# Retention of a two-layer decoder: rotated keys, state and queries in 16-bit parts, with the split and the state's spreading moved between engines

## The chip, the cores and the metric

The kernel runs on one core of one Trainium2 chip. The metric is the device time of one execution in microseconds. Of the kernel before there are three runs, and a profiled execution with its trace.

## The reference

A decoder of two layers on x of 2 x 1024 x 256 with a context of 2 x 154 x 192: a table-based attention, a cross attention and a mixture of experts; then a retention, a headed cross attention and a feed-forward part with sign weights. The change is in the retention alone. With 16 heads, key dimension 16 and head dimension 32 it computes, for tokens m and n of one sequence (positions m, n; `decay` per head):

```python
q = x @ q_w + q_b;  k = (x @ k_w + k_b) * SCALING;  v = x @ v_w + v_b;  g = x @ g_w + g_b
qr = q * cos + rotate_every_two(q) * sin            # the same for kr
qk = einsum('bhmd,bhnd->bhmn', qr, kr) * mask       # mask: tril(exp((m - n) * decay)) / sqrt(its row sum)
qk = qk / clip(abs(qk.sum(-1)), 1)
out = einsum('bhmn,bhnd->bhmd', qk, vr)
out = (out - mean) / sqrt(var + 1e-5)
out = (silu(g) * out) @ o_w + o_b
```

## The kernel before

`retention` runs 16 tiles of 128 tokens (`NT = 16`), 8 to a sequence (`TB = 8`). Within a tile the scores are formed and masked; what earlier tiles of the sequence give comes through a state `us` (per head 16 x 33: 32 values and a column of ones), decayed by `keep` and spread by head into `u`. Each engine has its own queue, written out by hand: a loop over steps s = -2 to 18 in which every function works on the tile that its argument names. Semaphores named after what is done (`rot_done`, `v_done`, ...) tie the engines together. Precise 32-bit work is done either with fp32 operands or with two fp16 parts, high and low, and three products.

What the queues hold per step, in order:

- TensorE: `score(s, 0)` (half of the heads, into `pss`), `weigh(s - 1)` (state product with `u`, attention by values, into `pso`), `qk(s + 2)` (projection into `psq`), `score(s, 1)`, `turn_qk(s + 1, 0)` (queries transposed into `ptr`), `output(s - 3)`, `turn_qk(s + 1, 1)` (keys), `values(s + 1)` (projection into `psv`), `delta(s)` (the tile's part of the state, into `psd`), `turn_z(s - 2)`, `turn_x(s + 4)`, `gates(s - 1)` (projection into the same `psv`). `pss` has one buffer, so `score(s, 1)` waits for `low(s, 0)`, and `score(s + 1, 0)` for `low(s, 1)`.
- VectorE: `low(s, 0)`, `x_center(s + 5)`, `gate(s - 2)`, `rotate(s + 2)`, `low(s, 1)`, `centre(s - 1)`, `state(s)`, `add(s - 3)`, `z_low(s - 2)`, `values_low(s + 1)`, `x_low(s + 4)`, and statistics for the next stage in some steps.
- ScalarE: `high(s, 0)`, `squares(s - 1)`, `high(s, 1)`, the copies of the turned queries and keys (L2859), `values(s + 1)` (a fp16 and a fp32 copy of the values, L2867 and L2868), `z_high(s - 2)`, `x_high(s + 4)`, `silu(s - 1)` (in place in `psv`, L2879).
- GpSimd: two selects for each half of the scores (`mask`, L2686), `power(s - 1)` (L2705), `expand(s)` (L2695: the state into `u`, four copies of it with all heads but one set to zero).

The rotation (L2779 to L2785) turns 256 queries and 256 keys per token with `cos` and `sin` and writes fp32 into `rot`, with 16 zeros behind each 16 values. Before, the scores (L2922) and the state's products (L2937, L3022) have fp32 operands. `values` runs on ScalarE; `values_low` subtracts the fp16 copy from the fp32 copy `v32`, both in SBUF, and `gates` waits for `v_done`, that is for ScalarE's second copy.

## Time and profile before

| | |
|---|---|
| median of three runs | 1028.42 us (1023.22 to 1030.12) |
| the profiled execution | 1025.94 us, of it 1024.1 us span |
| TensorE busy | 874.4 us, 85% of the span |
| VectorE busy | 784.2 us, 77% |
| ScalarE busy | 615.7 us, 60% |
| GpSimd busy | 372.5 us, 36% |
| mean granted TensorE clock | 0.949 |
| the retention | from about 506 to 720 us of the span |

Busy time is the time in which an engine's instructions ran; TensorE's are pipelined, so its rows overlap their successors and the distance between two starts is what a row costs. In a row of the timeline the first number is the start, the second how long the row lasted; "[1.29 <-ACT r_att L2852]" is idle time of the engine ahead of the row and what ended it. The names are `r_` with the tile's name of the code, `ra_` for tiles prepared ahead of the stage. On VectorE and ScalarE too neighbours overlap by about 0.1 us.

### The profile page before, as it was taken

Reading aid. Unit: us, or ns where it says so; the run is one execution under the profiler, and the core shown is the slowest. Engines: PE = TensorE matmul, PEld = TensorE weight load, DVE = VectorE, ACT = ScalarE, POOL = GpSimd, SP = SyncE. Lnnn points to the kernel's source line nnn. Section 1 sums busy time; section 2 is a strip of 40 time slices with the busy share of each in tenths; the row PEclk is TensorE's granted clock in tenths of the full one; section 3 lists DMA queues with packets and bytes.
Section 4 is the critical chain, followed back from the end, with each engine's and each line's share of the span. In section 5 each row is a group of like instructions: output and inputs, shape, how many; then the busy total and the mean of one; then the engine's idle time right before and its main releaser. Section 6 shows DMA issues by size and latency. Waiting matters only on the chain. (4 is left out here: it accounts for less than half of the span.)

```text
span 1024.1 us, 22180 instructions
## 1 busy us (share of the span) xinstructions
PE 874.4 (85%) x8762; PEld 579.5 (57%) x8762; DVE 784.2 (77%) x1460; ACT 615.7 (60%) x1108; POOL 372.5 (36%) x326
## 2 busy tenths in 40 slices
PE   1386878788488899999689999998799998999997
PEld 0122323232246555565356777776689975778786
DVE  8899989833788899887678899887577886667443
ACT  5578789887476554452155555554578865656431
POOL 1043435321247140000246667666144641224220
PEclk9998889898679899999899999999799999999999
DMA  5403232320420030000120000000200000000000
GB/s 148 83 1 48 36 54 32 48 37 1 135 72 1 2 135 1 1 2 1 58 111 1 3 2 2 2 3 2 73 2 2 2 1 1 2 12 11 12 22 31
DMA packets 21670, 30.47 MB, mean 30 GB/s; under 512 B 6000, under 2 KB 17982, under 8 KB 20416
## 3 DMA queue, kind: packets, MB, share of 16 engines
q1 hardware_dynamic: 18816, 26.44, 11.2%
q10 hardware_dynamic: 2752, 2.62, 0.9%
q8 instruction: 70, 1.15, 0.5%
q14 instruction: 32, 0.26, 0.1%
HBM read 18.56 MB, written 2.10 MB: 20 GB/s over the span
## 5 line engine op out<-in xcount | busy, mean ns | idle before, releaser
L589 ACT ACTIVATE t_pT<-t_sc 128x1536 f32<-128x1536 f32 x96 | 136.7, 1454 | 28.8 <-PE t_sc L696 28.5
L269 POOL TENSOR_SCALAR_AFFINE_SELECT t_pT<-t_pT 128x512 f32<-128x512 f32 x64 | 75.9, 1206 | 167.4 <-ACT t_pT L589 167.3
L696 PE MATMUL t_sc<-t_qk 32*128 32x512 f16 (+3 forms) x1152 | 89.1, 365 | 47.4 <-DMA t_qk<-t_sin_parts 26.6
L696 PEld LDWEIGHTS t_sc<-t_qk 32*128 32x128 f16 x1152 | 37.1, 99 | 107.0 <-issue 50.4
L2686 POOL TENSOR_SCALAR_AFFINE_SELECT r_att<-r_att 128x1024 f16<-128x1024 f16 x64 | 69.5, 1108 | 66.2 <-DVE r_att L2726 66.2
L717 PE MATMUL t_ot<-t_pT,t_v 128*17 128x512 f32 (+3 forms) x768 | 81.3, 535 | 11.3 <-DVE t_ou L433 5.1
L1983 PE MATMUL c_pso<-ck_VO,c_pT 128*128 128x256 f16 x480 | 55.0, 273 | 1.4 <-DVE c_pT L1824 1.4
L2726 DVE TENSOR_TENSOR r_att<-r_pss,r_att 128x1024 f16<-128x1024 f32 x32 | 39.1, 1221 | 20.2 <-ACT r_att L2852 20.2
L1983 PEld LDWEIGHTS c_pso<-ck_VO,c_pT 128*128 128x128 f16 x480 | 46.3, 98 | 6.7 <-DVE c_pT L1824 1.6
L2268 ACT ACTIVATE m_sg<-m_psg 128x512 f32<-128x512 f32 x32 | 19.1, 596 | 51.6 <-PE m_psg L2311 51.5
L2852 ACT CAST r_att<-r_pss 128x1024 f16<-128x1024 f32 x32 | 32.4, 1012 | 28.0 <-PE r_pss L2922 28.0
L1894 ACT ACTIVATE c_pt<-c_pss,c_mx 128x154 f32<-128x154 f32 x128 | 48.4, 415 | 1.1 <-DVE c_mx L1807 1.1
L2332 PE MATMUL m_acc<-gw_down,m_hp 128*128 128x256 f16 x384 | 47.2, 273 | 1.9 <-DVE m_hp L2224 1.4
L2948 PE MATMUL r_psv<-ra_w,ra_xT 128*128 128x512 f16 x192 | 46.8, 380 | 1.0 <-ACT r_v L2868 1.0
L2705 POOL TENSOR_TENSOR r_sm<-r_sm,ra_sm 128x16 f32<-128x16 f32 x16 | 46.3, 2895 | 3.6 <-DVE r_sm L2767 2.0
L717 PEld LDWEIGHTS t_ot<-t_pT,t_v 128*17 128x17 f32 x768 | 17.5, 102 | 51.8 <-issue 37.6
L1774 POOL TENSOR_TENSOR c_pn<-c_pt,c_tot 128x208 f32<-128x208 f32 x16 | 24.1, 1507 | 58.3 <-DVE c_tot L1814 58.3
L2332 PEld LDWEIGHTS m_acc<-gw_down,m_hp 128*128 128x128 f16 x384 | 36.9, 98 | 12.4 <-DVE m_hp L2224 2.0
L2922 PEld LDWEIGHTS r_pss<-r_qkT 32*128 32x128 f32 x512 | 31.0, 186 | 13.6 <-issue 11.2
L2922 PE MATMUL r_pss<-r_qkT 32*128 32x128 f32 x512 | 37.1, 283 | 1.0 <-DVE r_att L2726 1.0
L2859 ACT COPY r_qkT<-r_ptr 128x512 f32<-128x512 f32 x32 | 18.8, 588 | 29.7 <-PE r_ptr L2996 29.7
L1824 DVE TENSOR_TENSOR c_pT<-c_pst,c_pT 128x512 f16<-128x512 f32 (+1 forms) x48 | 28.7, 598 | 10.3 <-ACT c_pT L1905 9.4
(593 smaller groups left out, 2408.7 us busy)
## 6 DMA issues: line engine op xcount, KB each, us to landing
t_qk<-t_cos_parts SPq DMA_DIRECT2D x24, 128.0 KB, 5.4
t_qk<-t_sin_parts SPq DMA_DIRECT2D x24, 128.0 KB, 7.0
x<-in_x ACTq DMA_DIRECT2D x4, 512.0 KB, 7.3
out_x<-x SPq DMA_DIRECT2D x8, 256.0 KB, 2.1
r_rcos<-in_ret_cos SPq DMA_DIRECT2D x1, 1280.0 KB, 9.1
r_rsin<-in_ret_sin SPq DMA_DIRECT2D x1, 1280.0 KB, 10.6
t_qk<-t_cos_parts SPq DMA_DIRECT2D x16, 64.0 KB, 2.7
gw_raw<-in_gateT SPq DMA_DIRECT2D x1, 1024.0 KB, 7.6
```

What stands on the lines that cost most here:

```text
L269: last = g.affine_select(out=blk, in_=blk, compare_op=ALU.is_ge, fill=0.0, base=0, pattern=[[0, 4], [1, P]], channel_multiplier=-1)
L589: a.activation(pT[:, at:at + 3, :].rearrange("p a s -> p (a s)"), sc[s % 2][:], ACT.Exp, scale=CURVE * CURVE / math.sqrt(2 * DH)).then_inc ...
L696: last = t.matmul(sc[s % 2][:, 512 * k + at:512 * k + at + w], qk[r, g % 3, 1, of_k, P * i:P * i + P], qk[r, g % 3, 0, of_q, q0:q0 + w], s ...
L717: last = t.matmul(ot[j][32 * h:32 * h + DH + 1, 512 - w:512], v1[:, b, 4 * c + h, i, :], pT[:, (4 * slot + h) % RING, at:at + w], start=be ...
L1894: last = a.activation(pt[:, q, h, :], pss[:, k, n * CTX:n * CTX + CTX], ACT.Exp, bias=mx[:, q, 3 * k + n:3 * k + n + 1], scale=1.0, accum_ ...
L1983: last = mm(pso[:, 0:D], l, r, start=(n == 0), stop=(n == len(todo) - 1))
L2332: last = mm(acc[:, j, :], hp[:, k, ph_, P * j:P * j + P], dw[:, pw, D * e:D * e + D], start=(e == 0 and j % 2 == 0 and ph_ + pw == 0), sto ...
L2686: last = g.affine_select(out=blk, in_=blk, compare_op=ALU.is_ge, fill=0.0, base=0, pattern=[[0, 8], [1, P]], channel_multiplier=-1)
L2705: g.tensor_tensor(sm[:, q, 2, :], sm[:, q, 1, :], ahead.sm[:, 4, 0:1].broadcast_to((P, HR)), ALU.pow).then_inc(pow_done, 1)
L2726: v.tensor_tensor(att[:, t % 2, 1, 2 * j:2 * j + 2].rearrange("p h g m -> p (h g m)"), pss[:].rearrange("p j m -> p (j m)"), att[:, t % 2, ...
L2922: last = mm(pss[:, j, P * g:P * g + P], qkT[r, q, 1, g, :], qkT[r, q, 0, g, :], start=(g == 0), stop=True, skip_group_check=True)
L2948: last = mm(d, l, r, start=(i == 0), stop=(i == len(todo) - 1))
```

## The change

- The rotation's sum stays in `psq` in fp32. ScalarE copies it as fp16 into `rot` (`rotated_high`), VectorE subtracts that and writes the rest, fp16, beside it (`rotated_low`): 16 high values and 16 low ones stand where 16 values and 16 zeros stood. GpSimd writes a third plane of `rot` with the keys' two parts exchanged (`swap`).
- Scores are two fp16 products per head in place of one in fp32: keys (high, low) and keys (low, high), each with queries (high, low). Twelve fp16 transposes replace eight in fp32, and the keys' copy from `ptr` is 1024 wide.
- The state is split by GpSimd into fp16 parts `us16` (`split_state`), and `expand` moves from GpSimd to ScalarE: four operations with a scale per partition. The state product in `weigh` is two fp16 products for one in fp32; `delta` has four fp16 products for one in fp32.
- `v32` is gone. `values_low` reads `psv` itself, stands ahead of `state` and not behind `z_low`, and `gates` and the next `values` wait for `vlo_done`, where they waited for `v_done`.
- Ahead of the loop GpSimd no longer clears `rot`, and makes an fp16 identity.

```diff
         rfloor, keep = sb("rfloor", [P, TB, HR]), sb("keep", [P, 4])
-        rowtile = sb("rowtile", [P, 4])
+        rowtile, id16 = sb("rowtile", [P, 4]), sb("id16", [P, P], F16)
         rb = sb("rb", [P, 512])
-        rot = sb("rot", [P, ROTS, 2, HR, 2 * KD])
-        qkT = sb("qkT", [P, 2, 2, 4, P])
-        v32 = sb("v32", [P, 2, HR, VC])
+        rot = sb("rot", [P, ROTS, 3, HR, 2 * KD], F16)
+        qkT = sb("qkT", [P, 2, 3, 4, P], F16)
         v16 = sb("v16", [P, 2, 2, HR, VC], F16)
         att = sb("att", [P, 2, 2, 4, 4, P], F16)
-        u, us = sb("u", [P, 2, 4, 4, VC]), sb("us", [P, 2, 4, VC])
+        u, us = sb("u", [P, 2, 2, 4, 4, VC], F16), sb("us", [P, 2, 4, VC])
+        us16 = sb("us16", [P, 2, 2, 4, VC], F16)
+        ptr16 = ptr.bitcast(F16)
...
+            def split_state(t):
 
                 if inside(t) and t % TB != TB - 1:
                     g.wait_ge(kept_state, t + 1)
-                    wait(g, pv_done, t)
-                    g.tensor_tensor(u[:, (t + 1) % 2], us[:, t % 2].unsqueeze(2).broadcast_to((P, 4, 4, VC)),
-                                    rowtile[:].unsqueeze(1).unsqueeze(3).broadcast_to((P, 4, 4, VC)), ALU.mult).then_inc(u_done, 1)
+                    wait(g, u_done, t)
+                    own.link(g.tensor_copy(us16[:, t % 2, 0], us[:, t % 2]))
+                    g.tensor_tensor(us16[:, t % 2, 1], us[:, t % 2], us16[:, t % 2, 0], ALU.subtract).then_inc(us_split, 1)
                 elif inside(t):
                     g.wait_ge(kept_state, t + 1)
-                    g.tensor_copy(tiny[:], us[:, t % 2, 0, 0:1]).then_inc(u_done, 1)
+                    g.tensor_copy(tiny[:], us[:, t % 2, 0, 0:1]).then_inc(us_split, 1)
+
+            def swap(t):
+
+                if inside(t):
+                    keys, swap_ = rot[:, t % ROTS, 1], rot[:, t % ROTS, 2]
+                    g.wait_ge(rot_low, t + 1)
+                    g.tensor_copy(swap_[:, :, 0:KD], keys[:, :, KD:2 * KD])
+                    g.tensor_copy(swap_[:, :, KD:2 * KD], keys[:, :, 0:KD]).then_inc(swapped, 1)
 
             def power(t):
...
+                swap(s + 2)
                 power(s - 1)
-                expand(s)
+                split_state(s)
                 if s in (8, 14):
...
                     q = t % 2
                     v.wait_ge(vhi_done, t + 1)
-                    v.wait_ge(v_done, t + 1)
-                    v.tensor_tensor(v16[:, q, 1, :, 0:VD], v32[:, q, :, 0:VD], v16[:, q, 0, :, 0:VD], ALU.subtract).then_inc(vlo_done, 1)
+                    v.scalar_tensor_tensor(v16[:, q, 1, :, 0:VD], psv[:].rearrange("p (h d) -> p h d", h=HR), 1.0 / GAIN,
+                                           v16[:, q, 0, :, 0:VD], ALU.mult, ALU.subtract).then_inc(vlo_done, 1)
 
             def x_low(t):
                 if inside(t) and t >= FIRST:
@@ -2775,14 +2786,18 @@
                         if t == first:
                             v.wait_ge(done, n * 16)
                     v.wait_ge(qk_ready, t + 1)
-                    wait(v, rot_done, t)
+                    wait(v, rot_low, t)
                     own.mark(v.tensor_tensor(pair(rb[:])[:, :, 0], pair(psq[:])[:, :, 1], pair(sin)[:, :, 0], ALU.mult))
                     L(v.tensor_tensor(pair(rb[:])[:, :, 1], pair(psq[:])[:, :, 0], pair(sin)[:, :, 1], ALU.mult))
                     L(v.tensor_tensor(psq[:], psq[:], cos, ALU.mult))
-                    wait(v, k_turned, t - ROTS + 1)
-                    wait(v, d_ready, t - ROTS + 1)
-                    heads = lambda a: a.rearrange("p (a h d) -> p a h d", a=2, h=HR)
-                    v.tensor_tensor(rot[:, t % ROTS, :, :, 0:KD], heads(psq[:]), heads(rb[:]), ALU.add).then_inc(rot_done, 1)
+                    v.tensor_tensor(psq[:], psq[:], rb[:], ALU.add).then_inc(rot_done, 1)
+
+            def rotated_low(t):
+                if inside(t):
+                    parts = rot[:, t % ROTS, 0:2]
+                    v.wait_ge(rot_high, t + 1)
+                    v.tensor_tensor(parts[:, :, :, KD:2 * KD], psq[:].rearrange("p (a h d) -> p a h d", a=2, h=HR),
+                                    parts[:, :, :, 0:KD], ALU.subtract).then_inc(rot_low, 1)
 
             def state(t):
...
                 low(s, 1)
+                rotated_low(s + 2)
                 centre(s - 1)
+                values_low(s + 1)
                 state(s)
                 add(s - 3)
                 z_low(s - 2)
-                values_low(s + 1)
                 x_low(s + 4)
                 if 0 <= s - 3 < opening.SPANS[1][1]:
...
                         wait(a, pv_done, t - 1)
-                    a.copy(qkT[:, t % 2, n].rearrange("p g m -> p (g m)"), ptr[:]).then_inc(done, 1)
+                    which, wide = (slice(0, 1), 512) if n == 0 else (slice(1, 3), 1024)
+                    a.copy(qkT[:, t % 2, which].rearrange("p a g m -> p (a g m)"), ptr16[:, 0:wide]).then_inc(done, 1)
+
+            def rotated_high(t):
+                if inside(t):
+                    wait(a, k_turned, t - ROTS + 1)
+                    wait(a, d_ready, t - ROTS + 1)
+                    a.wait_ge(rot_done, t + 1)
+                    a.copy(rot[:, t % ROTS, 0:2, :, 0:KD], psq[:].rearrange("p (a h d) -> p a h d", a=2, h=HR)).then_inc(rot_high, 1)
+
+            def expand(t):
+
+                if inside(t):
+                    a.wait_ge(us_split, t + 1)
+                    wait(a, pv_done, t)
+                    if t == 0:
+                        a.wait_ge(s_c, 3)
+                    for h in range(4):
+                        last = a.activation(u[:, (t + 1) % 2, :, :, h, :], us16[:, t % 2], ACT.Copy, scale=rowtile[:, h:h + 1])
+                    last.then_inc(u_done, 1)
 
             def values(t):
...
                     a.mul(v16[:, t % 2, 0, :, 0:VD], heads, 1.0 / GAIN).then_inc(vhi_done, 1)
-                    a.mul(v32[:, t % 2, :, 0:VD], heads, 1.0 / GAIN).then_inc(v_done, 1)
 
             def z_high(t):
...
                 copy_turned(s + 1, 0, q_turned, q_copied)
+                rotated_high(s + 2)
                 copy_turned(s + 1, 1, k_turned, k_copied)
+                expand(s - 1)
                 values(s + 1)
...
                             r = slice(32 * h, 32 * h + 32)
-                            last = mm(pss[:, j, P * g:P * g + P], qkT[r, q, 1, g, :], qkT[r, q, 0, g, :], start=(g == 0), stop=True, skip_group_check=True)
+                            mm(pss[:, j, P * g:P * g + P], qkT[r, q, 1, g, :], qkT[r, q, 0, g, :], start=(g == 0), stop=False, skip_group_check=True)
+                        for j in range(2):
+                            h = 2 * half + j
+                            r = slice(32 * h, 32 * h + 32)
+                            last = mm(pss[:, j, P * g:P * g + P], qkT[r, q, 2, g, :], qkT[r, q, 0, g, :], start=False, stop=True, skip_group_check=True)
                     last.then_inc(scored, 1)
...
                         if t % TB:
-                            mm(pso[:, bank, c0:c0 + 4 * VC], qkT[:, q, 0, g, :], u[:, q, g].rearrange("p h d -> p (h d)"),
-                               start=(g % 2 == 0), stop=False, skip_group_check=True)
+                            for part in range(2):
+                                mm(pso[:, bank, c0:c0 + 4 * VC], qkT[:, q, 0, g, :], u[:, q, part, g].rearrange("p h d -> p (h d)"),
+                                   start=(g % 2 == 0 and part == 0), stop=False, skip_group_check=True)
                         for h in range(4):
...
                 if inside(t):
                     wait(t_, z_ready, t - 2)
-                    wait(t_, v_done, t)
+                    wait(t_, vlo_done, t)
                     project(t, psv[:], 512, v_psum)
 
             def gates(t):
                 if inside(t):
-                    upto(t_, v_done, t + 3)
+                    upto(t_, vlo_done, t + 3)
...
-                        t_.wait_ge(s_c, 4)
-                        t_.wait_ge(rot_done, t + 1)
+                        t_.wait_ge(s_c, 3)
+                        t_.wait_ge(rot_low, t + 1)
                         upto(t_, z_split, t - 3)
                         wait(t_, k_copied, t)
                     else:
                         t_.wait_ge(q_copied, t + 1)
-                    for g in range(4):
-                        last = t_.transpose(ptr[:, P * g:P * g + P], rot[:, t % ROTS, n, 4 * g:4 * g + 4, :].rearrange("p h d -> p (h d)"), ahead.ident[:])
+                        t_.wait_ge(swapped, t + 1)
+                    for which in (0,) if n == 0 else (1, 2):
+                        for g in range(4):
+                            to = P * (4 * (which // 2) + g)
+                            last = t_.transpose(ptr16[:, to:to + P], rot[:, t % ROTS, which, 4 * g:4 * g + 4, :].rearrange("p h d -> p (h d)"), id16[:])
                     last.then_inc(done, 1)
...
-                    t_.wait_ge(v_done, t + 1)
-                    t_.wait_ge(rot_done, t + 1)
+                    t_.wait_ge(vlo_done, t + 1)
+                    t_.wait_ge(swapped, t + 1)
                     wait(t_, kept_state, t)
                     for g in range(4):
-                        for h in range(4):
-                            last = mm(psd[32 * h:32 * h + 32, VC * g:VC * g + VC], rot[:, t % ROTS, 1, 4 * g + h, :], v32[:, q, 4 * g + h, :],
-                                      start=(g == 0), stop=True, skip_group_check=True)
+                        for which, part in itertools.product((1, 2), range(2)):
+                            for h in range(4):
+                                last = mm(psd[32 * h:32 * h + 32, VC * g:VC * g + VC], rot[:, t % ROTS, which, 4 * g + h, :], v16[:, q, part, 4 * g + h, :],
+                                          start=(g == 0 and which == 1 and part == 0), stop=(which == 2 and part == 1), skip_group_check=True)
                     last.then_inc(d_ready, 1)
```

How this changes the queues, at two places. On ScalarE, a step from the copy of the turned queries on; `r_qkT` are the turned queries and keys, `r_v16` and `r_v32` the values, `r_u` the spread state. Before:

```order
L2859 COPY r_qkT<-r_ptr 128x512 x2
L2867 ACTIVATE r_v16<-r_psv 128x16x32
L2868 ACTIVATE r_v32<-r_psv 128x16x32
L2874 CAST r_zT<-r_ptr 128x512
L2506 CAST ra_xT<-r_psq 128x2x128
```

After, the same place:

```order
L2876 COPY r_qkT<-r_ptr 128x512
L2883 CAST r_rot<-r_psq 128x32x16
L2876 COPY r_qkT<-r_ptr 128x1024
L2893 ACTIVATE r_u<-r_us16,r_rowtile 128x8x33 x4
L2902 ACTIVATE r_v16<-r_psv 128x16x32
L2908 CAST r_zT<-r_ptr 128x512
L2506 CAST ra_xT<-r_psq 128x2x128
```

The rotation's high part and the four spreading operations now stand ahead of the values' one copy. On VectorE, from the rotation's last sum to the end of the step; `r_att` is the scores' low part, `r_sm` belongs to `centre`, `r_us` to the state. Before:

```order
L2785 TENSOR_TENSOR r_rot<-r_psq,r_rb 128x32x16
L2726 TENSOR_TENSOR r_att<-r_pss,r_att 128x1024
L2762 SCALAR_TENSOR_TENSOR r_sm<-r_cen 128x16
L2763 TENSOR_TENSOR r_sm<-r_sm,r_rfloor 128x16
L2765 TENSOR_REDUCE r_sm<-r_sq 128x16
L2767 SCALAR_TENSOR_TENSOR r_sm<-r_sm 128x16
L2795 TENSOR_TENSOR r_us<-r_us,r_psd 128x132
L2798 TENSOR_TENSOR r_us<-r_us,r_keep 128x132
L2803 SCALAR_TENSOR_TENSOR x<-r_psd,x 128x256
L2809 TENSOR_TENSOR r_zT<-r_ptr,r_zT 128x512
L2734 TENSOR_TENSOR r_v16<-r_v32,r_v16 128x16x32
```

After:

```order
L2793 TENSOR_TENSOR r_psq<-r_psq,r_rb 128x512
L2737 TENSOR_TENSOR r_att<-r_pss,r_att 128x1024
L2799 TENSOR_TENSOR r_rot<-r_psq,r_rot 128x32x16
L2773 SCALAR_TENSOR_TENSOR r_sm<-r_cen 128x16
L2774 TENSOR_TENSOR r_sm<-r_sm,r_rfloor 128x16
L2776 TENSOR_REDUCE r_sm<-r_sq 128x16
L2778 SCALAR_TENSOR_TENSOR r_sm<-r_sm 128x16
L2744 SCALAR_TENSOR_TENSOR r_v16<-r_psv,r_v16 128x16x32
L2810 TENSOR_TENSOR r_us<-r_us,r_psd 128x132
L2813 TENSOR_TENSOR r_us<-r_us,r_keep 128x132
```

The rotation's low part is a new row behind the scores' low part, and the values' low part has moved up by four rows and reads `r_psv`.

## Rows read from the trace of the kernel before

**Rows 1.** Busy us by stretch: PE, PEld, DVE, ACT, POOL, then granted clock, DMA share, GB/s

```profile
575.00:610.00 35.00, 35.00 (x477) 25.67 (x476) 30.52 (x56) 18.82 (x31) 22.64 (x19) 1.00 0.01 2
...
862.50:875.00 12.50, 9.68 (x90) 8.04 (x91) 10.33 (x13) 8.93 (x14) 2.24 (x2) 1.00 0.00 0
```

**Rows 2.** Timeline of VectorE in one step: start us, us, engine, line, operation

```profile
588.60 1.22 DVE L2726 TENSOR_TENSOR r_att<-r_pss,r_att 128x1024 f16<-128x1024 f32 x1 [1.29 <-ACT r_att L2852]
589.74 0.40 DVE L2492 TENSOR_SCALAR ra_xn<-x,ra_sm 128x255 f32<-128x255 f32 x1
...
592.91 0.69 DVE L2785 TENSOR_TENSOR r_rot<-r_psq,r_rb 128x512 f32<-128x512 f32 x1
593.51 1.21 DVE L2726 TENSOR_TENSOR r_att<-r_pss,r_att 128x1024 f16<-128x1024 f32 x1
...
594.86 1.06 DVE L2763 TENSOR_TENSOR r_sm<-r_sm,r_rfloor 128x16 f32<-128x16 f32 x1
...
596.88 0.28 DVE L2795 TENSOR_TENSOR r_us<-r_us,r_psd 128x132 f32<-128x132 f32 x1
...
601.03 1.23 DVE L2726 TENSOR_TENSOR r_att<-r_pss,r_att 128x1024 f16<-128x1024 f32 x1 [1.29 <-ACT r_att L2852]
```

**Rows 3.** Timeline of TensorE in the same step

```profile
587.38 0.49 PE L2937 MATMUL r_pso<-r_u,r_qkT 128*128 128x132 f32 x2
587.71 0.46 PE L2941 MATMUL r_pso<-r_v,r_att 128*128 128x33 f16 x12
588.02 0.47 PE L2937 MATMUL r_pso<-r_u,r_qkT 128*128 128x132 f32 x2
...
597.32 1.47 PE L2948 MATMUL r_psv<-ra_w,ra_xT 128*128 128x512 f16 x6
598.72 1.16 PE L2922 MATMUL r_pss<-r_qkT 32*128 32x128 f32 x16
599.81 0.49 PE L2937 MATMUL r_pso<-r_u,r_qkT 128*128 128x132 f32 x2
```

**Rows 4.** Timeline of ScalarE in the same step

```profile
592.45 1.01 ACT L2852 CAST r_att<-r_pss 128x1024 f16<-128x1024 f32 x1 [1.31 <-PE r_pss L2922]
593.36 0.59 ACT L2859 COPY r_qkT<-r_ptr 128x512 f32<-128x512 f32 x1
...
596.18 0.60 ACT L2867 ACTIVATE r_v<-r_psv 128x512 f16<-128x512 f32 x1 [0.71 <-PE r_psv L2948]
596.67 0.59 ACT L2868 ACTIVATE r_v<-r_psv 128x512 f32<-128x512 f32 x1
...
598.83 0.58 ACT L2879 ACTIVATE r_psv<-r_psv 128x512 f32<-128x512 f32 x1 [0.81 <-PE r_psv L2948]
599.98 1.01 ACT L2852 CAST r_att<-r_pss 128x1024 f16<-128x1024 f32 x1 [0.57 <-PE r_pss L2922]
```

**Rows 5.** Timeline of GpSimd: the two selects beside `centre`

```profile
594.80 2.14 POOL L2686 TENSOR_SCALAR_AFFINE_SELECT r_att<-r_att 128x1024 f16<-128x1024 f16 x2 [2.66 <-DVE r_att L2726]
```

**Rows 6.** Timeline of VectorE at the stage's end, without selects on GpSimd

```profile
708.86 0.17 DVE L2763 TENSOR_TENSOR r_sm<-r_sm,r_rfloor 128x16 f32<-128x16 f32 x1
```

**Rows 7.** Timeline of TensorE in the table attention: fp16 products of 32 rows

```profile
129.98 0.83 PE L696 MATMUL t_sc<-t_qk 32*128 32x256 f16 x18 [0.83 <-ACT t_pT L589]
```

**Rows 8.** ScalarE by shape: from SBUF, with two and no SBUF scalars: xcount | busy, mean ns

```profile
L925 ACT ACTIVATE ce_room<-x,ce_room 128x256 f32<-128x256 f32 x16 | 10.0, 631 | 0.0
...
L1461 ACT ACTIVATE c_wk<-ce_room 128x256 f16<-128x256 f32 x1 | 0.4, 416 | 2.5 <-PEq L51 2.5
```

**Rows 9.** Timeline at the stage's start: second rotation's sum, first keys' copy

```profile
515.42 0.69 DVE L2785 TENSOR_TENSOR r_rot<-r_psq,r_rb 128x512 f32<-128x512 f32 x1
515.64 0.58 ACT L2859 COPY r_qkT<-r_ptr 128x512 f32<-128x512 f32 x1 [0.74 <-PE r_ptr L2996]
```

**Rows 10.** Timeline of VectorE: first low part of tile 0 and of tile 15

```profile
519.08 1.23 DVE L2726 TENSOR_TENSOR r_att<-r_pss,r_att 128x1024 f16<-128x1024 f32 x1 [0.26 <-ACT r_att L2852]
...
697.92 1.23 DVE L2726 TENSOR_TENSOR r_att<-r_pss,r_att 128x1024 f16<-128x1024 f32 x1 [1.96 <-ACT r_att L2852]
```

More of the change, by code:

```diff
@@ L2640, in retention @@
         s_norm, s_next, s_tab, s_v, s_g, s_c = sem("s_norm"), sem("s_next"), sem("s_tab"), sem("s_v"), sem("s_g"), sem("s_c")
-        names = ("qk_ready rot_done q_turned q_copied k_turned k_copied v_psum v_done "
+        names = ("qk_ready rot_done rot_high rot_low swapped us_split q_turned q_copied k_turned k_copied v_psum "
                  "g_psum silu_done scored hi_done lo_done kept_state masked vhi_done vlo_done d_ready u_done pv_done cen_done sq_done sq_used centred pow_done "
                  "z_ready z_turned zhi_done z_split o_ready x_added").split()
-        (qk_ready, rot_done, q_turned, q_copied, k_turned, k_copied, v_psum, v_done,
+        (qk_ready, rot_done, rot_high, rot_low, swapped, us_split, q_turned, q_copied, k_turned, k_copied, v_psum,
          g_psum, silu_done, scored, hi_done, lo_done, kept_state, masked, vhi_done, vlo_done, d_ready, u_done, pv_done, cen_done, sq_done, sq_used, centred, pow_done,
@@ L2670, in _ @@
             own = Tally(g, s_g)
-            g.memset(rot[:, :, :, :, KD:2 * KD], 0.0).then_inc(s_c, 1)
-            g.memset(v32[:, :, :, VD:VC], 1.0).then_inc(s_c, 1)
-            g.memset(v16[:, :, 0, :, VD:VC], 1.0).then_inc(s_c, 1)
-            g.memset(v16[:, :, 1, :, VD:VC], 0.0).then_inc(s_c, 1)
             own.link(g.memset(rowtile[:], 0.0))
@@ L2677, in _ @@
                 own.link(g.memset(rowtile[32 * h:32 * h + 32, h:h + 1], 1.0))
+            own.link(g.memset(id16[:], 0.0))
+            g.affine_select(out=id16[:], in_=id16[:], compare_op=ALU.not_equal, fill=1.0, base=0,
+                            pattern=[[-1, P]], channel_multiplier=1).then_inc(s_c, 1)
+            g.memset(v16[:, :, 0, :, VD:VC], 1.0).then_inc(s_c, 1)
+            g.memset(v16[:, :, 1, :, VD:VC], 0.0).then_inc(s_c, 1)
             ahead.power(g, 2)
@@ L2688, in mask @@
                     last.then_inc(masked, 1)
-            def expand(t):
+            def split_state(t):
                 if inside(t) and t % TB != TB - 1:
                     g.wait_ge(kept_state, t + 1)
-                    wait(g, pv_done, t)
-                    g.tensor_tensor(u[:, (t + 1) % 2], us[:, t % 2].unsqueeze(2).broadcast_to((P, 4, 4, VC)),
-                                    rowtile[:].unsqueeze(1).unsqueeze(3).broadcast_to((P, 4, 4, VC)), ALU.mult).then_inc(u_done, 1)
+                    wait(g, u_done, t)
+                    own.link(g.tensor_copy(us16[:, t % 2, 0], us[:, t % 2]))
+                    g.tensor_tensor(us16[:, t % 2, 1], us[:, t % 2], us16[:, t % 2, 0], ALU.subtract).then_inc(us_split, 1)
                 elif inside(t):
                     g.wait_ge(kept_state, t + 1)
-                    g.tensor_copy(tiny[:], us[:, t % 2, 0, 0:1]).then_inc(u_done, 1)
+                    g.tensor_copy(tiny[:], us[:, t % 2, 0, 0:1]).then_inc(us_split, 1)
[5 more added lines that the diff above has]
+                    g.tensor_copy(swap_[:, :, KD:2 * KD], keys[:, :, 0:KD]).then_inc(swapped, 1)
             def power(t):
@@ L2796, in state @@
                         new = us[:, t % 2]
-                    wait(v, u_done, t - 1)
+                    wait(v, us_split, t - 1)
                     v.tensor_tensor(us[:, t % 2], new, keep[:].unsqueeze(2).broadcast_to((P, 4, VC)), ALU.mult).then_inc(kept_state, 1)
@@ L2955, in qk @@
                     upto(t_, ahead.ready, t + (2 if t + 1 >= FIRST else 1))
-                    wait(t_, rot_done, t)
+                    wait(t_, rot_low, t)
                     project(t, psq[:], 0, qk_ready)
@@ L3009, in turn_x @@
                 if inside(t) and t >= FIRST:
-                    t_.wait_ge(rot_done, t - 1)
+                    t_.wait_ge(rot_low, t - 1)
                     ahead.turn(t_, t, psq)
@@ L3039, in _ @@
                 if s == NT:
-                    t_.wait_ge(rot_done, NT)
+                    t_.wait_ge(rot_low, NT)
                     t_.wait_ge(lo_done, 2 * NT)
```

## The prediction

> **What bounds the kernel now.** I read three views in this order: the busy times of the engines by stretch, the timeline of one step of the retention on each engine, and the waits at the ends of its gaps. The change touches nothing outside the retention, so only its steps count. In the stretch 575 to 610 us TensorE is busy all 35.00 us, VectorE 30.52, ScalarE 18.82 and GpSimd 22.64 [rows 1]. A step lasts 588.60 to 601.03 = 12.43 us on VectorE [rows 2], and also on TensorE (587.38 to 599.81) [rows 3]. TensorE runs its rows end to end, so its load is the step. VectorE's only stop in that step is 1.29 us before the first low part of the scores [rows 2]: about 11.1 us of load. Two engines are thus near full, and what ends a step after the change has to be worked out from the dependences and not from one engine's load.
>
> I count in T, us after the start of the low part `low(s, 0)` on VectorE (588.60). From [rows 2]: centring x stands at T 1.14, the rotation's last sum at T 4.31, `low(s, 1)` at T 4.91, and the state's first sum, which is the first row behind `centre`, at T 8.28.
>
> **What TensorE gives.** The four pairs of fp32 state products cost 0.33 each from start to start (587.38 to 587.71), and twelve fp16 products of 33 columns 0.31 (to 588.02), or 26 ns each [rows 3]. Eight fp16 state products in their place are about 0.46 instead of 1.32. Eight fp32 score products (16 instructions) take 1.09 per half [rows 3]. Their fp16 form isn't in the trace in this shape. Below it is bounded by 16 x 26 ns = 0.42, above by no gain at all, 1.09. The nearest row is 18 fp16 products of 32 rows and 256 columns in 0.83, three row groups at a time [rows 7]: 46 ns, so about 69 ns with two groups, 35 ns with 128 columns, 0.55 for sixteen. I take that. Twelve fp16 transposes against eight fp32 ones are a small gain. The state's update `delta` goes from 32 instructions to 64; at 26 ns each these would be 1.7 in all, so between nothing and 1.7 is added; I take 0.6. TensorE's step then falls by 0.9 + 1.1 - 0.6 = 1.4, to 11.0 (10.4 to 12.1 by the bounds of `delta`). Taken alone that would be worth some 20 us over the stage.
>
> A rule of the Trainium skill speaks to the scores. TensorE: Matmul & The Clock Gate, Part 3, says that products in distinct 32-row groups run concurrently; by it eight pairs of 128 columns are an estimated 0.45 us, against my 0.55. The sum would be 1.5 us lower over 15 steps. The fp32 rows here do not show full concurrency and I keep 0.55.
>
> **The new wait.** The values' 32-bit copy `v32` is gone, and VectorE now takes their low part from `psv` itself. So `gates(s - 1)`, which writes `psv`, waits for `values_low(s + 1)`; before it waited for ScalarE's second copy (596.67 + 0.59 = 597.26, gates at 597.32 [rows 3, 4]). Behind it in TensorE's queue stand the scores of the next step, and for these ScalarE's cast and VectorE's next `low` wait. That closes a loop through all of the step:
>
> From the start of `values_low`: 0.69 for an operation of 512 elements from PSUM (592.91 [rows 2]), 0.06 to TensorE, gates 1.40 (597.32 to 598.72 [rows 3]), scores 0.55, 0.17 until ScalarE starts (599.98 against 599.81 [rows 3, 4]) and 1.04 until VectorE's `low` starts (601.03 against 599.98 [rows 2, 4]). That is 3.91. ScalarE's silu, 0.58 long and 1.51 behind the start of gates [rows 4], ends just before its cast and doesn't add.
>
> **When can `values_low` start?** Two chains lead there.
>
> VectorE's own: `rotated_low` (0.6, new) is put between `low(s, 1)` and `centre`. But the product with `r_rfloor` in `centre` takes 1.06 at 594.86 and ends at 595.92, with the first of GpSimd's two selects of 594.80 (2.14 for both) [rows 2, 5], and 0.17 where GpSimd has nothing of the kind (708.86) [rows 6]. It was waiting 0.9 us, and the new 0.6 fits in that. So `centre` still ends at T 8.28 and `rotated_low` costs nothing. If this cover went, `values_low` would start 0.6 later on this chain. What the rows show is what the Trainium skill states in SBUF — State Buffer, section "Who interferes with whom": an instruction of VectorE with two SBUF inputs and one of GpSimd exclude each other for a whole instruction. Without that rule this chain would end at T 8.9 and not 8.28, and the sum would be 2.7 us higher.
>
> ScalarE's: the rotation ends at T 4.31 + 0.69 = 5.00. Then `rotated_high` starts at 5.06 and takes 0.50 from start to start (as 596.18 to 596.67 [rows 4]); the keys' copy, now 1024 wide, takes 0.91 by the cast of 1024 (592.45 to 593.36) [rows 4]; `expand`, moved from GpSimd, is four operations of 264 elements with a scale held in SBUF. No such row exists. From SBUF to SBUF, 256 elements take 0.416 with no operand of that kind and 0.631 with two [rows 8]; in between is 0.52, less the 0.1 by which neighbours overlap: 0.40 each, 1.6 in all (bounds 1.2 and 2.0). Then `values` 0.60 and 0.03. `values_low` can start at 5.06 + 0.50 + 0.91 + 1.6 + 0.63 = T 8.70. This chain is the later one.
>
> So a step lasts 8.70 + 3.91 = **12.61 us** against 12.43. TensorE waits some 1.5 us before gates and VectorE 1.1 before `low`; the gains of TensorE outside the scores are swallowed there, and so are the longer `delta` and the extra work of GpSimd (two swaps and two splits of the state in place of one product). GpSimd is busy 22.64 of 35 us [rows 1], so it has over 4 us a step to spare, and what it makes there is needed only in the next step.
>
> **The sum.** Nine full steps: 9 x 12.61 = 113.5. Three without centring of x (a row of 0.40 at 589.74 [rows 2], about 0.3 less with the overlap): 36.9. The step that begins at `low(1, 0)` has no gating (two operations of 512 elements, 1.3 less): 11.3; the one of 14 has no rotation, 11.3; that of 0 has neither gates nor spreading, 8.3. Together 181.3, where before 519.08 to 697.92 is 178.8 [rows 10]: **+2.5**. At the start the second projection waits for the first rotation's two parts, 1.3 later, and `rotated_high(1)` stands ahead of the first keys' copy: that copy started at 515.64 and can now start at 516.11 + 1.3 + 0.56 = 517.97. With it 1.01 long, scores 0.55 and the cast 1.04, the first `low` is at 520.8, not 519.08: **+1.8** [rows 9, 10]. At the end the last second score comes 0.5 sooner and the last weighing is 0.8 shorter: **-1.3**. Sum +3.0 on the profiled execution, whose own time is 1025.94: 1028.9. The median of the runs shown is 1028.42, 2.5 above that execution, so the forecast for a median is 1031.4, say 1031.
>
> **The rivals.**
> 1. *Slower: the loop is longer.* Each 0.1 us on ScalarE between the rotation and `values`, or on the scores, is 1.4 us. With 0.5 per spreading operation and fp16 scores no faster than fp32 (1.09) the step is 13.55, the kernel +16.5: 1045. It decides from 13.1 per step on. For it: no row shows either shape. Against: fp16 products of 32 rows are quick in [rows 7]. A fifth.
> 2. *Slower: the lock.* If `rotated_high` came more than 0.8 late, the product with `r_rfloor` would fall into the second select, and the last row of `centre` behind the swaps: `values_low` at about T 9.3, step 13.2, 1040. Against: it waits only for the rotation's sum and for the queries' copy, which stood at T 4.76 (593.36 [rows 4]) and comes sooner with shorter scores. 0.06.
> 3. *Slower: the clock falls,* since TensorE now pauses. In 862.5 to 875 it is busy 9.68 of 12.50 and still has 1.00 [rows 1]. Gates at the lower of the two levels, 1.2 for 2.4 GHz, in every step would be +1.4 a step, 1050. 0.04.
> 4. *Faster: TensorE stays the bound.* If `values_low` started by T 7.2, for instance because spreading and copies cost half my prices, the step would be TensorE's 11.2, -1.2 for 13 steps, and the kernel 1013. Against: even at 1.2 for spreading and 0.42 for scores the step is 12.1, because `centre` isn't over before T 8.28; that end is 1024. 0.10.
>
> **How the numbers follow.** My case has 0.60, the slower ones together 0.30, the faster one 0.10. A measurement of this kernel tells about 1% from no change, so 1018 to 1039 is "same"; my case lies in it, from 1024 to 1038. The range goes from 1021 to 1044: it takes in the cheap end with some of rival 4, and nearly all of rival 1. That gives faster 0.10, same 0.60, slower 0.30.
>
> **What the profile after would show.** Right: TensorE idle 1 to 2 us per step before the gates' product, put down to VectorE's low part of the values; TensorE busy near 88% of the steady stretch; steps of 12.5 to 12.7; `rotated_low` between `low` and `centre` with the product after it only 0.4 to 0.5 long; four spreading rows 0.40 apart; 16 score instructions in 0.5 to 0.6. Wrong: no idle before gates (rival 4), scores above 0.8 or spreading above 0.5 apart (rival 1), a granted clock under 1.00 in the steps (rival 3), or `centre` ending behind T 8.8 (rival 2).

## The result, and the profile after

The changed kernel takes 1043.33 us (median of 4 runs, 1040.12 to 1044.38) against 1028.84 for the kernel before (4 runs): a ratio of 1.0156, 95% interval 1.0111 to 1.020. It is slower, by 14.5 us where 3.0 were forecast: inside the range of 1021 to 1044, at its upper edge, but outside the band of 1% that the forecast of "same" meant. The profiled executions stand at 1042.99 and 1025.94.

Where these 17.05 us lie is read off VectorE's timeline. The first rotation's last sum begins 1.1 later than before (511.36 against 510.24), ahead of everything that the change touches. From it to the first `low` is 10.51 where it was 8.84: +1.7. From the first `low` to that of tile 15 is 195.1 (521.87 to 716.98) where it was 178.8 [rows 10]: **+16.3**. The stage's end is 2.0 shorter (19.39 against 21.43 from there to x's last update, at 736.37 and 719.35), and behind it nothing differs by 0.1. So the question is the fifteen steps. In order they last 8.01, 12.15, **14.46**, 13.11, **14.80**, 13.11, 13.12, 13.18, **14.53**, 13.11, **14.39**, 12.79, **14.26**, 12.86 and 11.23 us. There are two kinds: an ordinary one of 13.11, 0.5 above the forecast 12.61, and five that are another 1.3 to 1.7 longer.

**The ordinary step.** VectorE after, in the step from 597.51 to 610.63; it answers to [rows 2], with `low` now in L2737, `rotated_low` in L2799, `centre` in L2773 to L2778 and `values_low` in L2744 (start us, us, engine, line, operation):

```profile
602.43 1.21 DVE L2737 TENSOR_TENSOR r_att<-r_pss,r_att 128x1024 f16<-128x1024 f32 x1
603.56 0.68 DVE L2799 TENSOR_TENSOR r_rot<-r_psq,r_rot 128x512 f16<-128x512 f32 x1
604.16 0.69 DVE L2773 SCALAR_TENSOR_TENSOR r_sm<-r_cen 128x16 f32<-128x16 f32 x1
604.88 1.00 DVE L2774 TENSOR_TENSOR r_sm<-r_sm,r_rfloor 128x16 f32<-128x16 f32 x1
605.91 0.69 DVE L2776 TENSOR_REDUCE r_sm<-r_sq 128x16 f32<-128x512 f32 x1
606.63 0.17 DVE L2778 SCALAR_TENSOR_TENSOR r_sm<-r_sm 128x16 f32<-128x16 f32 x1
606.72 0.69 DVE L2744 SCALAR_TENSOR_TENSOR r_v<-r_psv,r_v 128x512 f16<-128x512 f32 x1
...
610.63 1.23 DVE L2737 TENSOR_TENSOR r_att<-r_pss,r_att 128x1024 f16<-128x1024 f32 x1 [1.09 <-ACT r_att L2868]
```

GpSimd beside it; its two selects answer to [rows 5]:

```profile
603.71 2.14 POOL L2688 TENSOR_SCALAR_AFFINE_SELECT r_att<-r_att 128x1024 f16<-128x1024 f16 x2 [2.65 <-DVE r_att L2737]
605.79 0.40 POOL L2708 COPY r_rot<-r_rot 128x256 f16<-128x256 f16 x1
```

`centre` has **three** operations with both inputs in SBUF. The second, L2774, was the prediction's. The third, L2778, starts when the selects and the copy of 605.79 are over, and lasts 0.17. The first, L2773, reads `cen` twice, as both inputs. Before the change it just slipped in ahead of the selects of 594.80. This row of the kernel before wasn't read for the prediction:

```profile
594.64 0.18 DVE L2762 SCALAR_TENSOR_TENSOR r_sm<-r_cen 128x16 f32<-128x16 f32 x1
```

With `rotated_low` ahead of it, it is issued 0.45 behind the start of the first select and lasts 0.69, to 604.85, that select's end (half of 2.14 behind 603.71). L2774 is then held until 605.88, beside the second select's end at 605.85. `values_low` starts at T 9.21.

ScalarE in that step, answering to [rows 4]: `rotated_high`, the keys' copy, the spreading, the values, and the cast ahead of the next `low`:

```profile
602.63 0.58 ACT L2883 CAST r_rot<-r_psq 128x512 f16<-128x512 f32 x1 [1.10 <-DVE r_psq L2793]
603.11 1.02 ACT L2876 COPY r_qkT<-r_ptr 128x1024 f16<-128x1024 f16 x1
604.01 1.74 ACT L2893 ACTIVATE r_u<-r_us,r_rowtile 128x264 f16<-128x264 f16 x4
605.65 0.59 ACT L2902 ACTIVATE r_v<-r_psv 128x512 f16<-128x512 f32 x1
...
609.58 1.01 ACT L2868 CAST r_att<-r_pss 128x1024 f16<-128x1024 f32 x1
```

TensorE, answering to [rows 3]: the gates, first and last of the eight pairs of scores, the state's products:

```profile
607.47 1.47 PE L2989 MATMUL r_psv<-ra_w,ra_xT 128*128 128x512 f16 x6 [2.39 <-DVE r_v L2744]
608.87 0.23 PE L2958 MATMUL r_pss<-r_qkT 32*128 32x128 f16 x2
...
609.27 0.22 PE L2962 MATMUL r_pss<-r_qkT 32*128 32x128 f16 x2
609.42 0.29 PE L2978 MATMUL r_pso<-r_u,r_qkT 128*128 128x132 f16 x2
```

The wait on which the forecast turned is there, in 14 of the steps. In the waits of TensorE (us in total, times, longest):

```profile
PE r_psv L2989 <- DVE r_v L2744: 31.8, 14, 2.5
```

**The long steps.** TensorE in one of them, the step of 14.80 from 569.60 to 584.40:

```profile
579.55 2.74 PE L2989 MATMUL r_psv<-ra_w,ra_xT 128*128 128x512 f16 x6 [2.39 <-DVE r_v L2744]
582.23 0.29 PE L2958 MATMUL r_pss<-r_qkT 32*128 32x128 f16 x2
...
583.20 0.40 PE L2978 MATMUL r_pso<-r_u,r_qkT 128*128 128x132 f16 x2
```

and the same stretch by windows (columns as in [rows 1]; the clock is the figure behind POOL's):

```profile
577.00:578.00 1.00, 0.17 (x2) 0.00 (x0) 0.97 (x2) 1.00 (x4) 1.00 (x2) 1.00 0.00 0
578.00:579.00 1.00, 0.00 (x0) 0.00 (x0) 0.96 (x3) 1.00 (x3) 0.64 (x3) 0.87 0.00 0
579.00:585.00 6.00, 5.45 (x66) 3.31 (x67) 3.19 (x8) 1.67 (x3) 3.57 (x3) 0.50 0.00 0
585.00:586.00 1.00, 1.00 (x20) 0.73 (x17) 1.00 (x3) 0.34 (x1) 0.30 (x1) 0.71 0.09 16
```

The clock falls while TensorE stands still ahead of the gates, from 1.00 to 0.50, that is from 2.4 to 1.2 GHz, and is back after 586. Gates last 2.74 instead of 1.47, the scores 0.97 instead of 0.55 (582.23 to 583.20), and both lie on the step's loop: 1.7 us.

### The profile page after: what moved, and what is told of

Its sections match the earlier page's. It is cut to its first block and busy times, and to the rows that moved or that the text cites. A ratio compares the mean times of both kernels' runs of the same rounds, so it can differ in the third digit from the quotient of the medians.

```text
span 1041.2 us, 23474 instructions
## 1 busy us (share of the span) xinstructions
PE 854.0 (82%) x9338; PEld 552.9 (53%) x9338; DVE 797.5 (77%) x1476; ACT 646.9 (62%) x1172; POOL 377.7 (36%) x372
## 5 line engine op out<-in xcount | busy, mean ns | idle before, releaser
L2989 PE MATMUL r_psv<-ra_w,ra_xT 128*128 128x512 f16 x192 | 53.2, 419 | 31.8 <-DVE r_v L2744 31.8
L2737 DVE TENSOR_TENSOR r_att<-r_pss,r_att 128x1024 f16<-128x1024 f32 x32 | 39.0, 1220 | 26.6 <-ACT r_att L2868 26.5
L2989 PEld LDWEIGHTS r_psv<-ra_w,ra_xT 128*128 128x128 f16 x192 | 18.1, 104 | 53.4 <-DVE r_v L2744 35.1
L1905 ACT CAST c_pT<-c_pst 128x512 f16<-128x512 f32 (+1 forms) x48 | 25.2, 528 | 16.9 <-PE c_pst L1973 16.9
L2311 PE MATMUL m_psg<-m_xT,gw_gate 128*128 128x512 f16 x144 | 35.0, 379 | 0.0
```

The costliest lines, as they stand in the source:

```text
L2737: v.tensor_tensor(att[:, t % 2, 1, 2 * j:2 * j + 2].rearrange("p h g m -> p (h g m)"), pss[:].rearrange("p j m -> p (j m)"), att[:, t % 2, ...
L2989: last = mm(d, l, r, start=(i == 0), stop=(i == len(todo) - 1))
```

## Experiments

In the diffs `-` is the changed kernel and `+` the experiment. The kernel before stands beside them with a median of 1027.32 (for experiments 1, 4, 8 and the 36 products of 3), 1027.29 (2, 5, 6, 7) and one run of 1027.38 (12 and 24 products). The expectations call experiment 1 e1 or the first edit, 5 e4 and 7 e8. "Steps" are distances between the `low(s, 0)`, read as above.

**1. The centre's first product alone** is put ahead of `rotated_low`, where it was before the change.

```
                 low(s, 1)
+                first_product(s - 1)
                 rotated_low(s + 2)
...
-                    L(v.scalar_tensor_tensor(low_, cen[:, q, :, VD], EPS, cen[:, q, :, VD], ALU.mult, ALU.mult))
```

> The changed kernel (1043.3 us, full steps of 13.11) with one move on VectorE: the first product of centre (the squared factor of the denominator, both inputs in SBUF) goes ahead of rotated_low, so that it starts about 0.15 us before GpSimd's select. Lock theory: in the changed kernel that product falls into the first select (0.69 long instead of 0.17) and the one with the floor into the second; now only the floor's product waits, for the end of the first select. centre ends 0.5 to 0.9 us earlier, values_low is then released by ScalarE at T 8.73, the step is 12.6 and the kernel 6 to 8 us faster: 1036. Rival, ScalarE's chain alone already sets the step: rows of centre change, the step stays 13.1 and the time 1043. Clock theory adds: with a pause of TensorE before gates shorter by 0.5, the steps at the lower clock may become fewer, at most another 7 us.

Measured: 1042.98 us, ratio 1.0137 (1.0115 to 1.0158), next to no gain where 1036 was expected. The ordinary step did come down, from 13.11 to 12.68. VectorE of this kernel:

```profile
602.95 0.18 DVE L2771 SCALAR_TENSOR_TENSOR r_sm<-r_cen 128x16 f32<-128x16 f32 x1
603.04 0.68 DVE L2804 TENSOR_TENSOR r_rot<-r_psq,r_rot 128x512 f16<-128x512 f32 x1
603.64 0.57 DVE L2779 TENSOR_TENSOR r_sm<-r_sm,r_rfloor 128x16 f32<-128x16 f32 x1
...
605.66 0.69 DVE L2744 SCALAR_TENSOR_TENSOR r_v<-r_psv,r_v 128x512 f16<-128x512 f32 x1 [0.40 <-ACT r_v L2908]
```

This is the picture that the forecast drew: the second product ends with the first select and `values_low` waits for ScalarE. But now seven steps, not five, have gates at the lower clock. The fifteen steps sum to 191.6: 3.6 less than in the changed kernel, but 8.9 more than in experiment 4, which has the same edit and no gates at the lower clock. So the clock takes back about 2 of 5.6 us. The other 3.6 are lost in the profiled execution outside the fifteen steps, 1.6 ahead of them and 2.0 behind; why is not shown.

**2. GpSimd's selects.** To see that they, and not a neighbour on VectorE, lengthen the centre, the second mask of each step is cut down. The scores of heads 2 and 3 of each group stay unmasked above the diagonal, so its result is not the reference's.

```
-                    for part in range(2):
+                    for part in range(1 if j else 2):
                         blk = att[:, t % 2, part, 2 * j:2 * j + 2].rearrange("p h g m -> p (h g) m")
+                        if j:
+                            blk = blk[:, 0:1, 0:16]
```

> GpSimd's second mask of a step, that of the heads 2 and 3, is cut from both parts of 128 x 8 x 128 to one piece of 128 x 1 x 16; those heads are left unmasked above the diagonal. Nothing on VectorE or ScalarE is touched. Theory (VectorE's operations with both inputs in SBUF are held up by the running select): the centre's first product takes 0.18 us instead of 0.69 and the second 0.17 instead of 1.00, though every other row ahead of them is the same; the centre ends at or before T 8.0 and a step of the ordinary kind comes to 12.6 to 12.7 us instead of 13.11. TensorE's pause ahead of the gates shortens to 1.9, where the first experiment still saw the lower clock in some steps, so some of them stay above 13. Rival (the first product is long because of rotated_low right ahead of it, or of the turned queries' late square): it still takes 0.69 and the step stays 13.1.

Measured (one run): 1044.04 us; ordinary steps of 12.67, nine steps with gates at the lower clock. VectorE, in the order of the changed kernel:

```profile
604.27 0.17 DVE L2775 SCALAR_TENSOR_TENSOR r_sm<-r_cen 128x16 f32<-128x16 f32 x1
604.48 0.36 DVE L2776 TENSOR_TENSOR r_sm<-r_sm,r_rfloor 128x16 f32<-128x16 f32 x1
```

0.17 for 0.69 and 0.36 for 1.00, with the same rows ahead: the selects are the cause. The second product was expected at 0.17. What is left of its wait ends with GpSimd's first copy of `swap`, which has moved up beside it:

```profile
604.41 0.40 POOL L2710 COPY r_rot<-r_rot 128x256 f16<-128x256 f16 x1 [0.40 <-DVE r_rot L2801]
```

**3. Work in TensorE's pause.** Products of a 128x128 identity, whose results are thrown away, go between `turn_x` and `gates`, released by `low(s, 1)`: 36, and then 12 and 24 of them.

```
                 turn_x(s + 4)
+                if 1 <= s <= NT - 2:
+                    t_.wait_ge(lo_done, 2 * s + 2)
+                    for i in range(36):
+                        mm(pss[:, 0, 0:P], id16[:], id16[:], start=True, stop=True, skip_group_check=True)
                 gates(s - 1)
```

> The changed kernel with 36 fp16 products of 128 columns (about 2.0 us) on TensorE between turn_x and gates in steps 1 to 14; they write the scores' idle bank, which the next scores overwrite, so nothing of the result changes. Clock theory: five of the changed kernel's steps are 14.3 to 14.8 long instead of 12.8 to 13.1, because TensorE's clock is at its lower level in them after the pause; without the pause all full steps are 13.1, the granted clock is 1.00 in the steps, and the kernel is 6 to 7 us faster, 1037. Lock theory alone expects no gain: the long steps stay and the time is 1043. If the extra products collide with the wait's end, each step is some 0.1 longer.

Measured: 1037.87 us, 1.0087 (1.0065 to 1.011). No step is long, the full ones are of the ordinary length, and the clock is 1.00 from 540 to 700. Adding work to the engine made the kernel 5.5 us faster.

> The changed kernel with 12 instead of 36 products put into TensorE's pause ahead of the gates (0.7 us of 2.4; their results are thrown away). Theory (what brings the lower clock is how long TensorE pauses ahead of the gates; a pause of 1.9 to 2.4 left in e1 and in the changed kernel had it in 5 to 8 of 14 steps, one of 1.7 in e4 in 3, one of 1.5 in e8 in none): about 1.7 us of pause is left, two to four steps at the lower clock, the others at 13.11; about 1039 to 1041. Rival (any work in the pause will do): all steps at 13.11, 1038. Rival (little work in it does nothing): five or more long steps, 1042 to 1044.

Measured (one run): 1037.24 us, no long step at all, where two to four were expected. A pause of 1.72 is left in most steps, and the clock holds through it. This is one execution; experiment 5 has as long a pause and three such steps of 14, so chance isn't excluded for the 12 products alone. TensorE of this kernel, and the window of the pause:

```profile
605.84 1.47 PE L2989 MATMUL r_psv<-ra_w,ra_xT 128*128 128x512 f16 x6 [1.72 <-DVE r_v L2744]
```

```profile
604.00:605.00 1.00, 0.12 (x3) 0.00 (x0) 0.93 (x2) 1.00 (x4) 0.91 (x3) 1.00 0.00 0
605.00:606.00 1.00, 0.16 (x1) 0.11 (x2) 0.97 (x3) 0.36 (x2) 0.74 (x1) 1.00 0.00 0
```

> The same with 24 products (1.4 us of the 2.4). Theory: 1.0 us of pause is left, all steps at 13.11, 1038. Rival (the pause must be filled): some steps of 14 or more.

Measured (one run): 1035.66 us, all steps ordinary. The fifteen steps sum to 187.9 with 12 and with 24 products, and to 188.3 with 36; beyond that the three times differ by what lies outside the steps. 195.1 less 187.9 is **7.2 us** for the clock.

**4. First product and 36 products together.**

> Both edits together. If lock and clock are two separate causes their gains add: steps of 12.6 throughout and 1029 to 1031, the forecast made before the result and the kernel before's own time (15 steps in 182 us where the changed kernel has 195). If the shorter pause of the first edit already keeps the clock up, this is no faster than the first edit alone, or slower by up to 0.1 us per step, since 36 products are then longer than the pause.

Measured: 1031.79 us, 1.0046 (1.0028 to 1.0064); full steps of 12.67, sum of the fifteen 182.7 against 181.3 forecast. With both causes taken out, the step is within 0.06 of the forecast's 12.61 and the time within 0.8 of its 1031.

**5. The second copy of the values is back** (`v32`), and the gates wait for ScalarE again.

```
-                    v.scalar_tensor_tensor(v16[:, q, 1, :, 0:VD], psv[:].rearrange("p (h d) -> p h d", h=HR), 1.0 / GAIN,
-                                           v16[:, q, 0, :, 0:VD], ALU.mult, ALU.subtract).then_inc(vlo_done, 1)
+                    v.wait_ge(v_done, t + 1)
+                    v.tensor_tensor(v16[:, q, 1, :, 0:VD], v32[:, q], v16[:, q, 0, :, 0:VD], ALU.subtract).then_inc(vlo_done, 1)
...
+                    a.mul(v32[:, t % 2], heads, 1.0 / GAIN).then_inc(v_done, 1)
...
-                upto(t_, vlo_done, t + 3)
+                upto(t_, v_done, t + 3)
```

> One part of the change is undone: ScalarE writes the values' second fp32 copy again (0.5 us behind the fp16 one), and VectorE takes the low part from that copy, so the gates, which overwrite psv, wait for ScalarE's copy and no longer for VectorE's values_low. Theory (the step's loop runs through the gates' wait for values_low, which ends at T 9.9): the gates begin at about T 9.3, the step of the ordinary kind falls from 13.11 to about 12.4 us, TensorE's pause shortens by 0.6, so fewer steps at the lower clock; together 1025 to 1035. Rival (VectorE's own chain sets the step, and the gates' wait only follows it): the step stays at 13.1 and the time at 1040 to 1045.

Measured: 1033.58 us, 1.0056 (1.0031 to 1.0081); ordinary steps of 12.43, three with gates at the lower clock. Undoing the new wait gives back 9.8 of the 14.5 us. That isn't the wait alone: the ordinary step is 0.68 shorter, and there are also two steps fewer at the lower clock. ScalarE and TensorE of this kernel, in a step with its first `low` at 595.33; the gates come at T 9.27, where they came at 9.96:

```profile
603.95 0.60 ACT L2906 ACTIVATE r_v<-r_psv 128x512 f32<-128x512 f32 x1
```

```profile
604.60 1.47 PE L2993 MATMUL r_psv<-ra_w,ra_xT 128*128 128x512 f16 x6 [1.70 <-ACT r_v L2906]
```

**6. The values ahead of the spreading on ScalarE, alone.**

```
-                expand(s - 1)
                 values(s + 1)
+                expand(s - 1)
```

> Only ScalarE's order is changed: the fp16 copy of the values stands ahead of the four spreading operations (1.7 us) instead of behind them. Theory (in the changed kernel values_low waits for VectorE's own centre, T 9.2, not for ScalarE, which would be ready at T 7.0 instead of 8.7): the ordinary step stays at 13.1, the time within 3 us of 1043. The spread columns end about 0.6 us later and are not waited for. Rival (ScalarE's chain, the forecast's own bound at 8.70, sets the step): it falls by up to 1.4 us a step, 1022 to 1030.

Measured: 1042.74 us, 1.0154 (1.0123 to 1.0184); ordinary steps of 13.11, five at the lower clock. ScalarE's values now stand at 602.53, and `values_low` still follows `centre`, at T 9.21 (first `low` at 596.02):

```profile
602.53 0.62 ACT L2902 ACTIVATE r_v<-r_psv 128x512 f16<-128x512 f32 x1
```

```profile
605.23 0.69 DVE L2744 SCALAR_TENSOR_TENSOR r_v<-r_psv,r_v 128x512 f16<-128x512 f32 x1
```

1.6 us of ScalarE's chain are worth nothing here. VectorE's chain binds, as said.

**7. First product and values ahead, together.**

> The two edits together: the centre's first product ahead of rotated_low, and the values' copy ahead of the spreading. Theory (two chains stand close behind each other: VectorE's lock at 9.2, ScalarE's at 8.7, and each hides what the other costs): neither bounds any more, the centre ends at about T 8.3 and values_low starts there, the ordinary step is 12.2 us; with a pause of about 1.5 us ahead of the gates there are no or few steps at the lower clock: 1024 to 1029. Rival (the pause is not what brings the lower clock): ordinary steps of 12.2, but five or more that are 1.3 or more longer, 1031 to 1037.

Measured: 1024.84 us (10 runs), 0.9975 (0.9962 to 0.9988); full steps of 12.18, none long. Two edits worth 0.4 and 0.6 us one by one are worth 18.5 together: the two chains stood 0.5 us apart. The pause is down to 1.46 and no step is at the lower clock, which is 7.2 of the gain.

**8. All three:** besides, `values_low` goes up to just behind the centre's second product, ahead of its reduction.

```
                     L(v.tensor_tensor(low_, low_, rfloor[:, t % TB, :], ALU.max))
+                values_low(t + 2)
+                if inside(t):
                     v.wait_ge(sq_done, t + 1)
...
-                values_low(s + 1)
```

> Not an undoing but what the theory says would break the loop: ScalarE copies the values ahead of spreading the state, VectorE does the first product of centre ahead of rotated_low, and values_low stands right behind centre's second product. values_low then starts at T 7.3 and gates at 8.1, where TensorE has just finished its other work: hardly a pause. The loop would be 11.2 us and VectorE's own load 11.1 to 11.4; steps of 11.3 to 11.7, no lower clock, 1012 to 1020 us, faster than both kernels. Rival: the last product of centre and GpSimd's second select collide and VectorE's load is over 12: 1025 to 1030. Rival two, gates and the loop through them do not set the step: 1036 as the first edit alone.

Measured: 1015.69 us (1014.57 to 1016.58), **0.9869** (0.9844 to 0.9894): faster than both kernels, most steps 11.4. `values_low` starts at T 7.49 (first `low` at 597.68), and TensorE's pause is 0.54:

```profile
605.17 0.69 DVE L2744 SCALAR_TENSOR_TENSOR r_v<-r_psv,r_v 128x512 f16<-128x512 f32 x1
```

```profile
605.92 1.47 PE L2996 MATMUL r_psv<-ra_w,ra_xT 128*128 128x512 f16 x6 [0.54 <-DVE r_v L2744]
```

## Why the prediction was wrong

**Right: what bounds the step.** The loop from `values_low` to the next `low`, said to be 3.91, is 606.72 to 610.63 = 3.91. Experiment 8 moved its start from T 9.21 to 7.49 and the ordinary step went from 13.11 to 11.40. Experiment 5 took `values_low` out of it, the gates came 0.69 sooner, and the step was 0.68 shorter. That TensorE's gain would be swallowed by its wait for VectorE is the 31.8 us of the wait above.

**Right: the prices that no row had.** Scores 0.55 for sixteen (608.87 to 609.42), as taken from the table attention's row. The rule of the Trainium skill weighed there, TensorE: Matmul & The Clock Gate, Part 3, gave an estimated 0.45; the row decides for 0.55. Spreading 0.41 from start to start (0.40 forecast), and `values` ended at T 8.73 (8.70). `delta`'s 64 instructions last 0.67 in all, its 32 before lasted 0.46, so they added 0.2 and not the 0.6 taken; TensorE's pause hides it.

**Wrong: "`centre` still ends at T 8.28 and `rotated_low` costs nothing."** The forecast had the mechanism, VectorE held until GpSimd's select ends, and applied it to the second product alone. It took the first one, which has two SBUF inputs as well, for free. Moving that first product by 0.6 made both selects count: the centre ended at T 9.2, behind ScalarE's 8.70 that was meant to be the later chain. Steps of 13.11 instead of 12.61, half a microsecond more also in the three without centring of x, and another 0.5 in the remaining three together: 187.9 less 181.3 is **+6.6 us**. Experiments 1 and 2 show the cause, and experiment 4 its size: 5.6 us less over the fifteen steps than with the 36 products alone (182.7 for 188.3). The 1.0 that is left was not taken apart; 0.06 a step of it is `values_low` at T 8.76 for 8.70, released by ScalarE. Rival 2 had this consequence (T 9.3, step 13.2, 1040) with 0.06, but hung it on a late `rotated_high`; that one came on time (602.63, T 5.1), so the lock needed no such help. What the Trainium skill states in SBUF — State Buffer, section "Who interferes with whom", that an instruction of VectorE with two SBUF inputs contends with one of GpSimd that reads SBUF, agrees with the rows (0.69 for 0.18): the failure was in asking which instructions it covers, and when each is issued.

**Wrong: "the clock falls", given 0.04.** The reason against it was one stretch, TensorE busy 9.68 of 12.50 at clock 1.00 [rows 1]. In 540 to 700 of the changed kernel it is busy 131.4 of 160, a higher share, at 0.94. A busy share over a stretch didn't tell this: the pause in each step did matter, but not by its length alone. TensorE's pause ahead of the gates, and how many of the 14 gates began at the lower clock:

| kernel | pause, us | gates at 1.2 GHz | clock, 540 to 700 |
|---|---|---|---|
| changed; experiment 6 | 1.7 to 2.5 | 5; 5 | 0.94; 0.93 |
| experiment 1; 2 | 1.8 to 2.0 | 7; 9 | 0.93; 0.91 |
| experiment 5 | 1.5 to 1.8 | 3 | 0.97 |
| 12 products | 1.6 to 1.8 | 0 | 1.00 |
| experiment 7 | 1.3 to 1.5 | 0 | 1.00 |
| 24 products; all three; 36 | 0.2 to 1.1 | 0 | 1.00 |

(The pause leaves out the last gates of the stage, where it is shorter.) It cost **7.2 us**: 1.7 in a step such as that of 14.80, where the rival had 1.4 and left out the scores. What decides in which step it falls is open: the shorter pause of experiment 1 has more such steps than the changed kernel's, and one of 1.7 has three or none, each count from one execution. That 36 products in the pause remove it is shown, in the profile and in the times of four runs. In the other rows of 0 it is gone too, but what they have in common was not tested.

**The rest.** The stage's start was +1.7 (+1.8 forecast), its end -2.0 (-1.3). That the start agrees is partly luck of this execution: in the profiles of the ten experiments the same stretch, from the first rotation's last sum to the first `low`, is 11.25 to 11.66 and not 10.51, so +2.4 to +2.8, and the first values' projection in it lasts about 2.8 at the lower clock, where it lasts 1.46 here. 1.7 + 2.5 + 6.6 + 7.2 - 2.0 is 16.0, and the 1.1 ahead of the stage makes the 17.1 measured between the two profiled executions. Of the rivals, no price in rival 1 came true, though its time did, and rival 4 needed `values_low` by T 7.2: at T 7.49 in experiment 8 the kernel was at 1015.69, against 1013.

## What to carry to other kernels

- When an instruction is put into a queue, every instruction behind it moves, not only the one known to wait. List all those that can be held up, with their inputs and their start against the other engine's start. Here it was a row that had escaped a select by 0.16 us.
- An engine that gets quicker and then waits in each step can lose its clock; here that cost 7.2 us. A repair can look nearly useless because a second chain stands close behind the first (0.4 and 0.6 us one by one, 18.5 together); try it with the repair of that chain before dropping it.
- An operation that frees PSUM for the next product should be issued as soon as its inputs are there. Three moves of single instructions turned +1.6% into -1.3%.

## What the runs showed of the hardware

- VectorE's instruction with the same SBUF tile as both inputs is held by a running GpSimd select like one with two tiles: 0.17 or 0.18 alone, 0.69 with half a select ahead.
- The 64 products of `delta`, with weights for 32 columns of the array and 33 columns long, run 9 ns apart (0.57 for their 64 weight loads), where full-width ones of 33 columns ran 26 ns apart [rows 3]:

```profile
603.43 0.57 PEld L3067 LDWEIGHTS r_psd<-r_v,r_rot 128*32 128x32 f16 x64 [0.42 <-issue]
```

- The clock fell within a pause of 2.4 us in a stage where TensorE was busy four fifths of the time, and stayed at 1.2 GHz for 6 us in which TensorE was busy 5.45. In the stretch of [rows 1] in which it was busy 0.77 of the time it did not fall.
